# The second layer's state-space stage: order of the next group's preparation

## The chip, the cores and the metric

The kernel runs on one core of one Trainium2 chip. The metric is the time of one execution on the device in microseconds (us), lower is better. A core has four compute engines that run their own instruction queues in order and meet at semaphores: TensorE (PE, with PEld for its weight loads), VectorE (DVE), ScalarE (ACT) and GpSimd (POOL).

## The reference, cut to what matters

The program is a decoder of four layers on 16 sequences of 128 tokens of width 128. The change lies in the first block of the second layer:

```
def _L1_attn_ref(x, ...):
    x_norm = _layernorm(x, ln_g, ln_b)
    x1 = x_norm @ w1_w + w1_b
    u = _silu(_depthwise_conv(x1, conv_w))        # 3 taps along time
    dt = softplus(u @ W_dt + b_dt); Bt = u @ W_B; Ct = u @ W_C
    # for each t, with 16 states n per channel d:
    #   h = exp(dt_t * A) * h + (dt_t * u_t) * B_t
    #   y_t = sum_n h * C_t
    x_ssm = y + u * D_skip
    v = _silu(x_norm @ v1_w + v1_b)
    return x_ssm * v @ w2_w + w2_b
x = _layernorm(x + _L1_attn_ref(x, ...))
```

## The kernel before

`l1_attn` takes the 16 sequences in NG = 4 groups of G = 4, so that a tile is 128 channels by GT = 512 positions. A group has N = 16 states; each is one slot, so that NS = 64 slots run through k, with g = k // 16 and n = k % 16. All loops are written out by hand for each engine; the text order is the queue order.

**A slot.** On TensorE `row_pair(k + 1)` broadcasts the row of B and that of C of the next state into PSUM (lines 3383 and 3387; the B row needs the drive two slots back done, the C row needs ScalarE's copy two slots back), and `add(k - 2)` sums `read` into the PSUM bank `total` (3395, an fp32 product and so two passes). ScalarE copies the C row to SBUF (`c_move`, 3491) and makes the decays exp(dt * A) two slots ahead (`decay_`, 3484, three buffers). VectorE multiplies the B row by `du` (`drive_`, 3563) and scans (`scan`, 3570). GpSimd multiplies the scanned state by the C row (`read_`, 3679). There is one `drive` bank, so drive and scan alternate.

**The preparation of the next group** hangs in fixed slots n of the present one: layer-norm moments on VectorE (`pre_moments`, 3531 and 3533), reciprocal root on GpSimd (`pre_norm`), `pre_scale` on VectorE (3540), transposes on TensorE (`turn_x`, 3336), copy to `xT` (`move_x`, 3439), the convolution as three shifted products and a bias product (`conv`, 3346 and 3349), the gate (`gate`, 3353), their copies into `ug` and a silu over both halves (`move_ug`, 3446 and 3448, and `silu`, 3454), B and C (`bc`, 3359), which are split in three bf16 parts by `split_first` (3457), `split_rest` (3549), `split_mid` (3463, 3464) and `split_low` (3653), and dt (`dt_dot`, 3363; `soften`, 3468 to 3476: bias, absolute value, exponential, logarithm; `softplus_` on VectorE, 3553), at last `du` on GpSimd (`delta_u`, 3659). The functions silu, exponential and logarithm each need their table in ScalarE, and a table load stands in the queue wherever it changes.

**The end of a group** hangs in slots of the next: `skip` (3577) reads `total`, which must be done before the first `add` of the new group may write it; `gated` (3664) on GpSimd; `project_out` (3370, 3371) on TensorE in slots 4 and 5; `moments` and `scale` of the output layer norm on VectorE in slots 7 and 9. The PSUM results of preparation and projection share two banks, `spare`; the list `order` gives who uses which, and a user waits for the release of the one two places ahead.

**Head and tail.** The head prepares group 0 with nothing beside it; the tail finishes group 3. No DMA is issued in the stage.

## Time and profile before

| | us |
|---|---|
| median of 3 runs | 5305.53 |
| lowest and highest run | 5302.63, 5315.38 |
| profiled execution | 5310.23 |
| its span on the core | 5308.4 |
| mean granted clock of TensorE, share of full | 0.91 |
| busy: TensorE, VectorE, ScalarE, GpSimd | 4389.6, 3540.4, 2773.1, 2456.5 |
| the edited stage, from 2239.4 | 232 |

The span is that of the whole program. The stage is read by its own stretches: the first scan starts at 2271.6, the first drive of groups 1, 2 and 3 at 2310.8, 2361.3 and 2412.2, the last scan ends at 2453.6. An idle time in square brackets stands before the instruction that ended it, with who released it. Clock values are shares of full speed; TensorE has the two levels 1.2 and 2.4 GHz (0.50 and 1.00).

### The profile page before, as it was taken

To read this page: it belongs to the slowest core of one execution; us is meant where nothing else is said; L and a number is where in the kernel's file an instruction comes from. 1 tells how busy PE (TensorE), PEld (TensorE's weight loads), DVE (VectorE), ACT (ScalarE), POOL (GpSimd) and SP (SyncE) were. 2 spreads that over 40 slices of the span, in tenths; PEclk is the share of its full clock that TensorE was granted. 3 is DMA by queue.
4 is the path that set the end of the run, shared out by engine and by line. 5 is a ranking of instruction groups with operands and counts; after the bars stand their busy time and mean duration, and the time that the engine had idled before them with its cause. 6 is when DMAs were issued, how large, how long until landed. Compare 5 with 4: busy or idle time off the path is not lost. (4 is left out here: it accounts for less than half of the span.)

```text
span 5308.4 us, 109154 instructions
## 1 busy us (share of the span) xinstructions
PE 4389.6 (83%) x42474; PEld 2700.0 (51%) x42474; DVE 3540.4 (67%) x6848; ACT 2773.1 (52%) x4991; POOL 2456.5 (46%) x2333
## 2 busy tenths in 40 slices
PE   8768999999999999677864888887798879985779
PEld 6545666666666666424632343433365444423445
DVE  4347777777777777476466999999764426646646
ACT  4326676666666666464334656565464415543322
POOL 7536666666665666343044766676533310001100
PEclk9779999999999999877966999999999959996889
DMA  1000100101011000000000000000000000003000
GB/s 24 16 28 15 33 20 21 33 20 29 24 29 24 16 16 20 10 0 2 13 0 15 1 1 0 1 0 1 15 1 1 6 13 6 16 1 75 5 21 7
DMA packets 92006, 76.99 MB, mean 15 GB/s; under 512 B 30999, under 2 KB 74280, under 8 KB 90728
## 3 DMA queue, kind: packets, MB, share of 16 engines
q1 hardware_dynamic: 89447, 68.95, 5.2%
q8 instruction: 342, 5.60, 0.4%
q0 software_dynamic: 2048, 1.05, 0.1%
q14 instruction: 169, 1.38, 0.1%
HBM read 40.18 MB, written 1.18 MB: 8 GB/s over the span
## 5 line engine op out<-in xcount | busy, mean ns | idle before, releaser
L4220 POOL TENSOR_TENSOR l_attn_read<-l_attn_state,l_attn_c_rows 128x1024 f32<-128x1024 f32 x256 | 604.4, 2362 | 291.4 <-DVE l_attn_state L4122 171.6
L2595 PE MATMUL psum<-l_ffn_wq,l_ffn_xsT 128*128 128x512 f32 x1152 | 607.9, 610 | 106.9 <-DVE l_ffn_t L2870 101.5
L3006 POOL TENSOR_TENSOR l_ffn_t<-l_ffn_t 128x512 f32<-128x512 f32 x384 | 486.8, 1268 | 421.3 <-DVE l_ffn_t L2870 416.6
L3842 PE MATMUL psum<-l_attn_read,ident 128*128 128x512 f32 x1024 | 490.6, 597 | 7.7 <-DVE l_attn_yz L4130 5.3
L2866 DVE TENSOR_TENSOR l_ffn_t<-psum,l_ffn_tab 128x512 f32<-128x512 f32 x384 | 260.7, 679 | 326.2 <-ACT l_ffn_sq L2746 307.2
L3012 POOL TENSOR_TENSOR l_ffn_t<-l_ffn_t,l_ffn_ss 128x512 f32<-128x512 f32 x384 | 400.4, 1043 | 62.8 <-DVE l_ffn_ss L2885 62.6
L2746 ACT ACTIVATE l_ffn_sq<-psum 128x512 f32<-128x512 f32 x384 | 225.4, 587 | 290.4 <-PE psum L2595 288.1
L4122 DVE TENSOR_TENSOR_SCAN l_attn_state<-l_attn_decay,psum 128x1024 f32<-128x1024 f32 x144 | 328.9, 2284 | 4.5
L2643 PEld LDWEIGHTS psum<-l_ffn_pT,l_ffn_v 64*64 64x64 f32 x3072 | 231.1, 133 | 167.2 <-ACT l_ffn_pT L2768 132.2
L3998 ACT ACTIVATE l_attn_decay<-l_attn_dt,l_attn_a 128x1016 f32<-128x1016 f32 x256 | 292.9, 1145 | 37.4 <-DVE l_attn_state L4119 34.0
L4023 ACT COPY l_attn_c_rows<-psum 128x512 f32<-128x512 f32 x256 | 149.5, 584 | 297.5 <-PE psum L3833 261.0
L2595 PEld LDWEIGHTS psum<-l_ffn_wq,l_ffn_xsT 128*128 128x128 f32 x1152 | 182.5, 192 | 236.4 <-DVE l_ffn_t L2870 187.3
L2217 ACT ACTIVATE l_attn_pT<-psum 128x512 f32<-128x512 f32 x320 | 173.7, 595 | 243.2 <-PE psum L2115 172.1
L3833 PE MATMUL psum<-l_attn_parts,pick 96*128 96x512 bf16 x456 | 170.1, 390 | 136.8 <-DVE psum L4105 87.9
L4119 DVE TENSOR_TENSOR_SCAN l_attn_state<-l_attn_decay,psum 128x512 f32<-128x512 f32 x224 | 261.7, 1208 | 30.9 <-PE psum L3872 29.0
L2643 PE MATMUL psum<-l_ffn_pT,l_ffn_v 64*64 64x96 f32 (+1 forms) x3072 | 257.6, 233 | 21.2 <-ACT l_ffn_pT L2768 18.9
L3842 PEld LDWEIGHTS psum<-l_attn_read,ident 128*128 128x128 f32 x1024 | 195.7, 193 | 140.6 <-issue 117.0
L4105 DVE TENSOR_TENSOR psum<-psum,l_attn_du 128x1024 f32<-128x1024 f32 x200 | 246.6, 1233 | 26.5 <-POOL l_attn_du L4197 4.6
L2870 DVE TENSOR_TENSOR l_ffn_t<-psum,l_ffn_tab 128x512 f32<-128x512 f32 x384 | 261.4, 681 | 0.0
L2879 DVE TENSOR_REDUCE l_ffn_ss<-l_ffn_sq 128x8 f32<-128x512 f32 x384 | 259.5, 676 | 0.0
L3017 POOL TENSOR_TENSOR l_ffn_p<-l_ffn_p,l_ffn_sm 128x512 f32<-128x512 f32 x192 | 200.1, 1042 | 120.6 <-DVE l_ffn_sm L2902 120.6
L2643 PE MATMUL psum<-l_ffn_pT,l_ffn_vx 64*64 64x96 f32 (+1 forms) x3072 | 255.0, 233 | 0.0
(922 smaller groups left out, 11237.2 us busy)
## 6 DMA issues: line engine op xcount, KB each, us to landing
l_ffn_vx<-l_ffn_v SPq DMA_DIRECT2D x192, 128.0 KB, 2.3
l_ffn_wq<-in_L_ffn_Wqkv SPq DMA_DIRECT2D x6, 1536.0 KB, 6.2
l_xattn_toep<-s4d_taps SPq DMA_DIRECT2D x4, 2048.0 KB, 17.9
l_ffn_wo<-in_L_ffn_Wo SPq DMA_DIRECT2D x6, 512.0 KB, 3.9
l_ffn_w<-in_L_ffn_W SPq DMA_DIRECT2D x6, 341.0 KB
l_ffn_w<-in_L_ffn_w SPq DMA_DIRECT2D x3, 512.0 KB, 4.2
x_all<-in_x SPq DMA_DIRECT2D x4, 256.0 KB, 5.3
l_attn_k<-l_attn_dense_k POOLq DMA_DIRECT2D x64, 16.0 KB, 1.8
```

The lines of the kernel that those rows point to most:

```text
L2595: nc.tensor.matmul(ring[it % 2], xsT[:, n % 2, m % G, :], w, start=True, stop=True).then_inc(itemed, 1)
L2643: last = nc.tensor.matmul(OT[r, i * T + to:i * T + to + n], kinds[par][r, 4 * c + i, :], pT[r, i, at:at + n], start=(to == 0), stop=True, ...
L2866: nc.vector.tensor_tensor(t1[:, m % G, i, :].rearrange("p (h d) -> p h d", d=dh), dots.rearrange("p (h d) -> p h d", d=dh), rows(tab[:, z, ...
L2870: nc.vector.tensor_tensor(t2[:, x % 3, :].rearrange("p (h s d) -> p h s d", s=2, d=32), swapped_halves(dots, 8), tab[:, z, 2 * k + 1, :].r ...
L2879: nc.vector.reduce_sum(ss[:, m % G, 8 * i:8 * i + 8], sq[:, x % 2, :].rearrange("p (h d) -> p h d", d=dh), AX).then_inc(ss_ready, 1)
L3006: nc.gpsimd.tensor_tensor(t1[:, m % G, i, :], t1[:, m % G, i, :], t2[:, x % 3, :], ALU.add).then_inc(added, 1)
L3012: nc.gpsimd.tensor_tensor(t1[:, m % G, i, :].rearrange("p (h d) -> p h d", d=dh), t1[:, m % G, i, :].rearrange("p (h d) -> p h d", d=dh), ...
L3842: last = nc.tensor.matmul(total[:, h * GT:(h + 1) * GT], K.ident[:], read[:, k % 3, h * GT:(h + 1) * GT], start=(n == 0), stop=(n == N - 1 ...
L3998: nc.scalar.activation(decay[:, k % 3, :, :, 1:T], dt[:, g % 2, :].rearrange("p (h g t) -> p h g t", h=2, g=G)[:, :, :, 1:T], ACT.Exp, sca ...
L4119: nc.vector.tensor_tensor_scan(state[:, k % 3, at], decay[:, k % 3, h, :, :].rearrange("p g t -> p (g t)"), drive[:, at], 0.0, ALU.mult, A ...
L4122: nc.vector.tensor_tensor_scan(state[:, k % 3, :], decay[:, k % 3, :, :, :].rearrange("p h g t -> p (h g t)"), drive, 0.0, ALU.mult, ALU.a ...
L4220: nc.gpsimd.tensor_tensor(read[:, k % 3, :].rearrange("p (h n) -> p h n", h=2), state[:, k % 3, :].rearrange("p (h n) -> p h n", h=2), row ...
```

## The change

The preparation of the next group moves within the 16 slots:

| step | slot before | slot after |
|---|---|---|
| moments and reciprocal root of the next group | 0 and 1 | all groups in the head |
| `pre_scale` | 2 | head for group 1, then 13 of the group before |
| transposes, `move_x` | 3, 4 | 0, 1 |
| `conv` on TensorE, copy | 5 and 6, 7 | 1 and 2, 3 |
| `gate`, gate copy and silu | 7, 8 | 3, 4 |
| `dt_dot`, `soften` | 11, 12 | 6, 7 and 8 (logarithm) |
| `softplus_`, `delta_u` | 14, 14 | 10, 10 |
| `bc`, `split_first`, `split_rest`, `split_mid` | 10, 11, 12, 12 | 8, 9, 11, 11 |
| `skip`, `gated` | 3, 3 | 2, 2 |

In the head u gets a silu of its own ahead of the gate's copy, dt comes ahead of B and C, and VectorE makes `du` of group 0. The copy into `ug` waits, from group 2 on, for `gated` of two groups back, whose buffer it takes. The moments' tiles hold 16 sequences in place of 4; `pre_norm` runs twice, over 4 and over 12 of them. The diff, without the bodies of `pre_moments`, `pre_scale` and `pre_norm`, which change in their indices and waits alone:

```diff
...
         spare = (K.bank[6], K.bank[7])
-        order = [("x", 0), ("conv", 0), ("gate", 0), ("parts", 0), ("dt", 0)]
+        order = [(n, 0) for n in ("x", "conv", "gate", "dt", "parts")]
         for g in range(NG):
             if g + 1 < NG:
-                order.append(("x", g + 1))
+                order += [(n, g + 1) for n in ("x", "conv", "gate")]
             if g:
...
             if g + 1 < NG:
-                order += [(n, g + 1) for n in ("conv", "gate", "parts", "dt")]
+                order += [(n, g + 1) for n in ("dt", "parts")]
         order.append(("out", NG - 1))
...
                     ps = claim(use["parts", g])
-                    pe.wait_ge(ug_ready, g + 1)
                     pe.wait_ge(prepared, 2)
...
                 def dt_dot(g):
-                    nc.tensor.matmul(claim(use["dt", g]), wdt[:], ug[:, g % 2, 0, :], start=True, stop=True).then_inc(filled, 1)
+                    ps = claim(use["dt", g])
+                    pe.wait_ge(ug_ready, g + 2 if g else 1)
+                    nc.tensor.matmul(ps, wdt[:], ug[:, g % 2, 0, :], start=True, stop=True).then_inc(filled, 1)
 
...
                 gate(0)
-                bc(0)
                 dt_dot(0)
+                bc(0)
                 row_pair(0)
...
                         continue
-                    if g + 1 < NG and n == 3:
-                        turn_x(g + 1)
+                    if g + 1 < NG:
+                        if n == 0:
+                            turn_x(g + 1)
+                        if n in (1, 2):
+                            conv(g + 1, 2 * (n - 1))
+                            conv(g + 1, 2 * (n - 1) + 1)
+                        if n == 3:
+                            gate(g + 1)
                     if g and n in (4, 5):
...
                     if g + 1 < NG:
-                        if n in (5, 6):
-                            conv(g + 1, 2 * (n - 5))
-                            conv(g + 1, 2 * (n - 5) + 1)
-                        if n == 7:
-                            gate(g + 1)
-                        if n == 10:
-                            bc(g + 1)
-                        if n == 11:
+                        if n == 6:
                             dt_dot(g + 1)
+                        if n == 8:
+                            bc(g + 1)
                 for i in range(G):
...
                     ps = take(n)
+                    if g >= 2:
+                        act.wait_ge(y_ready, g - 1)
                     if i == 0:
...
 
+                def silu_first(i):
+                    wait_moved(act, use[("conv", "gate")[i], 0])
+                    nc.scalar.activation(ug[:, 0, i, :], ug[:, 0, i, :], ACT.Silu).then_inc(ug_ready, 1)
+
                 def silu(g):
...
 
-                def soften(g):
+                def soften(g, i):
                     n = use["dt", g]
-                    nc.scalar.activation(dt[:, g % 2, :], take(n), ACT.Identity, bias=cl[:, 3:4]).then_inc(moved[n % 2], 1)
...
+                    if i == 0:
+                        nc.scalar.activation(dt[:, g % 2, :], take(n), ACT.Identity, bias=cl[:, 3:4]).then_inc(moved[n % 2], 1)
...
+                        nc.scalar.activation(tmp[:], tmp[:], ACT.Exp, scale=-1.0).then_inc(soft_step, 1)
+                    else:
+                        act.wait_ge(soft_step, 3 * g + 2)
+                        nc.scalar.activation(tmp[:], tmp[:], ACT.Ln, bias=1.0).then_inc(soft_step, 1)
...
                 move_ug(0, 0)
+                silu_first(0)
                 move_ug(0, 1)
-                silu(0)
+                silu_first(1)
+                soften(0, 0)
                 split_first(0)
+                soften(0, 1)
                 split_mid(0)
-                soften(0)
                 act.wait_ge(prepared, 3)
...
                     if g + 1 < NG:
-                        if n == 4:
+                        if n == 1:
                             move_x(g + 1)
-                        if n == 7:
+                        if n == 3:
                             move_ug(g + 1, 0)
-                        if n == 8:
+                        if n == 4:
                             move_ug(g + 1, 1)
                             silu(g + 1)
-                        if n == 11:
+                        if n == 7:
+                            soften(g + 1, 0)
+                        if n == 8:
+                            soften(g + 1, 1)
+                        if n == 9:
                             split_first(g + 1)
-                        if n == 12:
+                        if n == 11:
                             split_mid(g + 1)
-                            soften(g + 1)
 
...
                 nc.vector.tensor_scalar(a[:], a[:], -1.0, None, ALU.mult).then_inc(prepared, 1)
+                for g in range(1, NG):
+                    pre_moments(g)
+                pre_scale(1)
                 split_rest(0)
                 softplus_(0)
+                dve.wait_ge(dt_ready, 1)
+                nc.vector.tensor_tensor(du[:, 0, :], dt[:, 0, :], ug[:, 0, 0, :], ALU.mult).then_inc(du_ready, 1)
                 for k in range(NS):
...
                     drive_(k)
-                    if g + 1 < NG:
-                        if n == 0:
-                            pre_moments(g + 1)
-                        if n == 2:
-                            pre_scale(g + 1)
                     if g:
-                        if n == 3:
+                        if n == 2:
                             skip(g - 1)
...
                     if g + 1 < NG:
-                        if n == 12:
-                            split_rest(g + 1)
-                        if n == 14:
+                        if n == 10:
                             softplus_(g + 1)
+                        if n == 11:
+                            split_rest(g + 1)
+                    if g + 2 < NG and n == 13:
+                        pre_scale(g + 2)
                     scan(k)
...
                 pre_norm(0)
+                pre_norm(1)
                 split_low(0)
-                delta_u(0)
                 for k in range(NS):
                     g, n = k // N, k % N
-                    if g + 1 < NG and n == 1:
-                        pre_norm(g + 1)
                     read_(k)
                     if g:
-                        if n == 3:
+                        if n == 2:
                             gated(g - 1)
...
                     if g + 1 < NG:
+                        if n == 10:
+                            delta_u(g + 1)
                         if n == 12:
                             split_low(g + 1, k)
-                        if n == 14:
-                            delta_u(g + 1)
                 gated(NG - 1)
```

On TensorE, from slot 3 of group 1 on before, with the projection of group 0 (3370, 3371) behind the transposes (3336):

```order
L3383 MATMUL psum<-l_attn_parts,pick 128x512
L3387 MATMUL psum<-l_attn_parts,pick 128x512
L3395 MATMUL psum<-l_attn_read,ident 128x512
L3336 MATMUL psum<-ident,l_attn_xn 128x128 x4
L3383 MATMUL psum<-l_attn_parts,pick 128x512
L3387 MATMUL psum<-l_attn_parts,pick 128x512
L3395 MATMUL psum<-l_attn_read,ident 128x512
L3370 MATMUL psum<-l_attn_w,l_attn_yz 128x128
L3371 MATMUL psum<-l_attn_b,ones 128x128
```

Now, from slot 0 of group 1 on; `xTp` and `wk` are the convolution's input and taps:

```order
L3384 MATMUL psum<-l_attn_parts,pick 128x512
L3388 MATMUL psum<-l_attn_parts,pick 128x512
L3396 MATMUL psum<-l_attn_read,ident 128x512
L3336 MATMUL psum<-ident,l_attn_xn 128x128 x4
L3384 MATMUL psum<-l_attn_parts,pick 128x512
L3388 MATMUL psum<-l_attn_parts,pick 128x512
L3396 MATMUL psum<-l_attn_read,ident 128x512
L3346 MATMUL psum<-l_attn_xTp,l_attn_wk 128x512 x2
L3384 MATMUL psum<-l_attn_parts,pick 128x512
```

The transposes and the first two taps now stand ahead of the group's own first `add`, which follows this piece (the two 3396 here sum the last states of group 0). Line numbers of the changed kernel are higher by 1 to 15.

On ScalarE, slots 12 and 13 of group 0 before; `low` and `parts` are the split of B and C, `dt` and `tmp` the softplus:

```order
L3491 COPY l_attn_c_rows<-psum 128x512
L3484 ACTIVATE l_attn_decay<-l_attn_dt,l_attn_a 128x4x127
L3463 CAST l_attn_low<-l_attn_rest 32x512
L3464 CAST l_attn_parts<-l_attn_rest 32x512
L3468 ACTIVATE l_attn_dt<-psum,l_attn_cl 128x512
L3472 ACTIVATE l_attn_tmp<-l_attn_dt 128x512
L3474 ACTIVATE l_attn_tmp<-l_attn_tmp 128x512
L3476 ACT_TABLE_LOAD
L3476 ACTIVATE l_attn_tmp<-l_attn_tmp 128x512
L3491 COPY l_attn_c_rows<-psum 128x512
L3484 ACT_TABLE_LOAD
L3484 ACTIVATE l_attn_decay<-l_attn_dt,l_attn_a 128x4x127
```

Now, slots 7 to 9:

```order
L3477 ACTIVATE l_attn_dt<-psum,l_attn_cl 128x512
L3481 ACTIVATE l_attn_tmp<-l_attn_dt 128x512
L3483 ACTIVATE l_attn_tmp<-l_attn_tmp 128x512
L3501 COPY l_attn_c_rows<-psum 128x512
L3494 ACTIVATE l_attn_decay<-l_attn_dt,l_attn_a 128x4x127
L3486 ACT_TABLE_LOAD
L3486 ACTIVATE l_attn_tmp<-l_attn_tmp 128x512
L3501 COPY l_attn_c_rows<-psum 128x512
L3494 ACT_TABLE_LOAD
L3494 ACTIVATE l_attn_decay<-l_attn_dt,l_attn_a 128x4x127
L3465 CAST l_attn_parts<-psum 96x512
```

The seven instructions of one slot are now spread over slots 7 to 11, with C's copy and a decay between them.

On VectorE, head before, from the negated `a` to the first scan:

```order
L3611 TENSOR_SCALAR l_attn_a<-l_attn_a 128x16
L3549 TENSOR_TENSOR l_attn_rest<-psum,l_attn_parts 96x512
L3553 SCALAR_TENSOR_TENSOR l_attn_dt<-l_attn_dt,l_attn_tmp 128x512
L3563 TENSOR_TENSOR psum<-psum,l_attn_du 128x512
L3531 BN_STATS l_attn_pre_stats<-x_all 128x6 x4
L3533 BN_AGGR l_attn_pre_mean<-l_attn_pre_stats 128x2 x4
L3570 SCALAR_TENSOR_TENSOR l_attn_state<-l_attn_decay,psum 128x512
```

Now, from the last moments to the first drive:

```order
L3544 BN_STATS l_attn_pre_stats<-x_all 128x6 x4
L3546 BN_AGGR l_attn_pre_mean<-l_attn_pre_stats 128x2 x4
L3554 TENSOR_SCALAR l_attn_xn<-x_all,l_attn_pre_mean,l_attn_pre_rstd 128x128 x4
L3563 TENSOR_TENSOR l_attn_rest<-psum,l_attn_parts 96x512
L3567 SCALAR_TENSOR_TENSOR l_attn_dt<-l_attn_dt,l_attn_tmp 128x512
L3632 TENSOR_TENSOR l_attn_du<-l_attn_dt,l_attn_ug 128x512
L3577 TENSOR_TENSOR psum<-psum,l_attn_du 128x512
```

The moments left the place between the first drive and the first scan, and `du` is VectorE's.

## Rows read from the trace of the kernel before

**Rows 1.** Busy time by stretch: the head and the four groups.

```profile
core 0: us, PE busy (x) PEld busy (x) DVE busy (x) ACT busy (x) POOL busy (x), PEclk, DMA share, GB/s
2239.40:2271.60 32.20, 15.29 (x24) 4.86 (x24) 7.58 (x37) 16.43 (x21) 5.97 (x7) 0.55 0.00 0
...
2271.60:2310.80 39.20, 31.44 (x78) 11.92 (x78) 33.01 (x39) 31.52 (x48) 22.67 (x20) 0.86 0.00 1
...
2310.80:2361.30 50.50, 37.01 (x98) 15.21 (x97) 39.35 (x60) 31.50 (x48) 26.23 (x24) 0.83 0.00 0
...
2361.30:2412.20 50.90, 37.52 (x100) 15.61 (x99) 39.35 (x61) 31.60 (x48) 26.32 (x24) 0.83 0.00 0
...
2412.20:2453.60 41.40, 30.93 (x79) 11.87 (x78) 35.10 (x46) 17.78 (x29) 22.57 (x19) 0.87 0.00 1
```

**Rows 2.** Timeline of VectorE, group 1: start and duration in us, instruction, [idle before].

```profile
2313.01 1.19 DVE L3570 TENSOR_TENSOR_SCAN l_attn_state<-l_attn_decay,psum 128x512 f32<-128x512 f32 x1
...
2314.31 0.70 DVE L3563 TENSOR_TENSOR psum<-psum,l_attn_du 128x512 f32<-128x512 f32 x1
...
2316.37 0.70 DVE L3563 TENSOR_TENSOR psum<-psum,l_attn_du 128x512 f32<-128x512 f32 x1
...
2318.87 1.21 DVE L3570 TENSOR_TENSOR_SCAN l_attn_state<-l_attn_decay,psum 128x512 f32<-128x512 f32 x1
...
2324.19 0.70 DVE L3563 TENSOR_TENSOR psum<-psum,l_attn_du 128x512 f32<-128x512 f32 x1 [1.52 <-PE psum L3383]
...
2334.86 0.70 DVE L3563 TENSOR_TENSOR psum<-psum,l_attn_du 128x512 f32<-128x512 f32 x1 [2.72 <-PE psum L3383]
...
2337.79 1.19 DVE L3570 TENSOR_TENSOR_SCAN l_attn_state<-l_attn_decay,psum 128x512 f32<-128x512 f32 x1
...
2361.33 0.70 DVE L3563 TENSOR_TENSOR psum<-psum,l_attn_du 128x512 f32<-128x512 f32 x1 [1.78 <-PE psum L3383]
```

**Rows 3.** Waits in the stage, 2230 to 2480 us: total, times, longest.

```profile
DVE psum L3563 <- PE psum L3383: 19.3, 13, 2.7
...
DVE l_attn_dt L3553 <- ACT l_attn_tmp L3476: 10.9, 4, 6.6
...
DVE psum L3563 <- POOL l_attn_du L3659: 5.1, 3, 1.8
```

**Rows 4.** Timeline of TensorE in groups 1 and 3.

```profile
2321.68 2.04 PE L3395 MATMUL psum<-l_attn_read,ident 128*128 128x512 f32 x2 [6.01 <-DVE l_attn_yz L3577]
...
2327.34 1.02 PE L3395 MATMUL psum<-l_attn_read,ident 128*128 128x512 f32 x2
...
2327.77 0.19 PEld L3370 LDWEIGHTS psum<-l_attn_w,l_attn_yz 128*128 128x128 f32 x1 [0.24 <-issue]
...
2329.76 0.39 PE L3383 MATMUL psum<-l_attn_parts,pick 96*128 96x512 bf16 x1
...
2358.28 0.63 PE L3383 MATMUL psum<-l_attn_parts,pick 96*128 96x512 bf16 x1
...
2360.84 0.46 PE L3383 MATMUL psum<-l_attn_parts,pick 96*128 96x512 bf16 x1
...
2442.61 1.80 PE L3395 MATMUL psum<-l_attn_read,ident 128*128 128x512 f32 x2
```

**Rows 5.** Timeline of the head, all engines.

```profile
2253.04 0.58 ACT L3446 COPY l_attn_ug<-psum 128x512 f32<-128x512 f32 x1 [6.58 <-PE psum L3349]
...
2259.96 0.69 DVE L3549 TENSOR_TENSOR l_attn_rest<-psum,l_attn_parts 96x512 f32<-96x512 f32 x1 [14.92 <-ACT l_attn_parts L3457]
...
2261.37 1.15 POOL L3653 TENSOR_TENSOR l_attn_parts<-l_attn_rest,l_attn_low 32x512 bf16<-32x512 f32 x1 [18.04 <-ACT l_attn_low L3463]
...
2263.32 1.28 ACT L3474 ACT_TABLE_LOAD   x1
...
2264.62 0.63 ACT L3474 ACTIVATE l_attn_tmp<-l_attn_tmp 128x512 f32<-128x512 f32 x1
...
2271.63 1.19 DVE L3570 TENSOR_TENSOR_SCAN l_attn_state<-l_attn_decay,psum 128x512 f32<-128x512 f32 x1
```

More of the change, by code:

```diff
@@ L3285, in l1_attn @@
         xn = sb("xn", [128, G, D])
[L3286 to L3288 removed]
+        pre_stats = sb("pre_stats", [128, NB, 6])
+        pre_mean = sb("pre_mean", [128, NB, 2])
+        pre_rstd = sb("pre_rstd", [128, NB])
         xT = sb("xTp", [128, G, T + TAPS - 1])
```

62 lines of the change are left out of this document (27 added, 35 removed).

## The prediction

> **What bounds the kernel now.** The page comes first: a span of 5308.4 us over all four layers, of which the edited stage is a small part. The view of busy time by stretch then gives its size [rows 1]: a head of 32.2 us, four groups of 39.2, 50.5, 50.9 and 41.4 us, and a tail of 18.1 us. In the groups VectorE is busy 33.0 of 39.2, 39.4 of 50.5, 39.4 of 50.9 and 35.1 of 41.4 us. No other engine sets the pace on average, though TensorE is close behind (37.0 of 50.5 us, at a mean granted clock of 0.83 of full speed). A slot on VectorE is a drive product (0.70) and a scan (1.19 to 1.22); undisturbed, drive follows drive after 2.06 us (2314.31 to 2316.37) [rows 2]. So 64 slots are 132 us, and the most that better order can win is the waits and extras between them.
>
> The view of waits says who stops VectorE [rows 3]: B's rows from TensorE (19.3 us in 13 waits), the logarithm for the softplus from ScalarE (10.9, of which 6.6 in the head), `du` from GpSimd (5.1 in 3). The timeline of group 1 shows where [rows 2]: four waits, 1.52 to 2.72 us at the ends, before the drives of slots 4 to 7 (6.3 us in all), and 1.78 before the next group; one of 1.31 before the softplus lies between. The first four have one origin. TensorE stood idle for 6.01 us until `skip` in slot 3 had read the total [rows 4], was then at half clock (1.2 GHz, a pair of passes in 2.04 us against 1.02 later at 2.4 GHz), and had projection and convolution to do in the same slots. Group 2 repeats this (six waits, 9.7 us); group 3, with only the projection, has four waits of 4.5 us.
>
> **The change part by part.** I count each stretch anew: undisturbed VectorE time plus the waits I still expect. A scan starts 0.73 us after its drive; what more it takes is the extra's price [rows 2]: `pre_moments` 1.5 (2310.8 to 2313.01), `pre_scale` 1.8 (2316.37 to 2318.87), output moments 2.2 (2334.86 to 2337.79); `scale`, four operations of the same kind as `pre_scale`, 1.8; `skip`, `split_rest` and softplus, one 512-column operation each, 0.6.
>
> *Head.* The new ScalarE queue is convolution copy, table load, silu of u, gate copy, silu of gate, then dt. From the copy's start at 2253.04 [rows 5]: copy 0.58, load 1.28, half a silu 0.63 (as the 128x512 exponential at 2264.62) gives 2255.55; the dt product at half clock, 2.04 [rows 4], gives 2257.6; bias, absolute value, load, exponential 0.69 + 0.63 + 1.28 + 0.63 gives 2260.85; first rounding of B and C 0.58, load and logarithm 1.91 give 2263.3. The low part needs 0.61 on ScalarE and 1.15 on GpSimd (2265.15), the first B row 0.58 and its drive 0.70 (2266.45); ScalarE's second cast, load and decay end at 2266.6. Softplus and `du`, now on VectorE (0.69 each), end at 2264.8 and are covered. The first scan starts at 2266.65 against 2271.63: **5.0 us won**, with 1.5 either way for the new interleaving. The moments of the three other groups (3 x 1.7) and one `pre_scale` lie on a VectorE that waits 14.92 us there [rows 5]: free; should that cover be missing, 7 us.
>
> *Group 0.* Clean: 15 x 2.06 + 1.33 to the next group's first drive, + 0.6 + 0.6 + one `pre_scale` 1.78 = 35.2 us. The waits for softplus (1.68) and `du` (1.77) go, since both are made by slot 10. New waits come on TensorE. In slot 1 it stands before the convolution until ScalarE has moved xT (after two decays and two C rows, about 2270.8), in front of B's row of slot 3. The two taps cost 1.7 us at full clock and 3.4 at half, so that row comes 1.0 or 2.8 us late, and the tap and bias of slot 2 cost 1.3 to 3.7 more. Bounds 2.3 and 6.5. Before, TensorE came to full clock some 8 us after its first row, in group 0; the new order has it at work from 2265 on, so that about half of the excess remains: 3.6. Sum 38.8 against 39.2: **0.4 won**.
>
> *Group 1.* Clean: 16 x 2.06 = 33.0, skip 0.6, moments 2.2, scale 1.8, 0.6 + 0.6, `pre_scale` of group 3 1.78: 40.6. `skip` comes a slot earlier and the pre-moments are gone, so TensorE waits for the total some 3 us less. Following the queues from the last scan's end: xT moved at 3.5, two taps to 5.2, first `add` 5.6 to 6.5 (`skip` ends at 5.45), tap and bias to 8.3, B of slot 4 at 8.7 (due 8.8), gate to 10.5, half the projection to 13.8 (1.99 us a slot, 2327.77 to 2329.76 [rows 4]), so B of slot 6 is 1.2 us late, and B of slot 7 again 1.2. That is 2.4 us at full clock; if the group starts at half clock, as before at 2321.68, about 6. The light slots speak for some of that: in group 3 a pair of passes took 1.80 us at 2442.61, after `scale` on VectorE had left TensorE without work [rows 4]. I take 3.5. Sum 44.1 against 50.5: **6.4 won**.
>
> *Group 2.* The same without `pre_scale`: 38.8 + 3.5 = 42.3 against 50.9: **8.6 won**.
>
> *Group 3.* 32.9 + 0.6 + 2.2 + 1.8 = 37.5; the projection alone fits in the slack (bounds 0 and 1.0, I take 0.5): 38.0 against 41.4: **3.4 won**.
>
> *Added wait.* From group 2 on, the copy of the convolution into `ug` waits for `gated` two groups back. It can start at about 7.4 after the last scan; GpSimd ends read and gate at 6.7 + 1.27 + 1.27 = 9.3. So ScalarE stands 1.9 us, with C's row of slot 4 and a decay behind it. The decay of slot 7, after the silu and its two loads, ends at 16.9 and is due at about 18: covered by 1 to 3 us of run-ahead. Uncovered it is in the first rival. Tail and head's first half are unchanged: 0.
>
> **Sum:** 5.0 + 0.4 + 6.4 + 8.6 + 3.4 = 23.8 us. The profiled execution took 5310.2 (span 5308.4), 4.7 above the median of the runs, 5305.5, which itself lies between 5302.6 and 5315.4. 5305.5 - 23.8 = 5281.7. With all TensorE waits at their low ends (2.3 + 2.4 + 2.4 + 0 = 7.1 instead of 11.1) and the head at its best it is 29.3 us, with all at their high ends (6.5 + 6 + 6 + 1 = 19.5) and the head at its worst 13.9.
>
> A page against a row. In the trace a table load takes 1.28 us, no idle time stands before it, and the next activation starts 1.30 after it (2263.32, 2264.62) [rows 5]. The Trainium skill, ScalarE: Activation LUTs, What ACT_TABLE_LOAD costs, adds 1.38 us of drain to the 1.28. That is a sentence on the page alone: by it the four loads of a group would make ScalarE 5.5 us busier, and the clumps in slots 4 and 8 would reach the scans; I would estimate some 8 us less gain, about 5290 (an estimate from the page's figure). The rows speak against it.
>
> **Rivals.** *The wait moves to ScalarE.* Silu, gate copy and two loads now fall in slots 3 to 5, where TensorE, too, is fullest, and in groups 1 and 2 the new wait precedes them. If `gated` ends a slot and a half later than I count (3 us), the decay of slot 7 and C's row of slot 5 are late, TensorE, which takes its rows in order, holds B back, and some 5 us are lost in each of groups 1 and 2 and 3 in group 0: gain 23.8 - 13 = 10.8, 5294.7. For it: ScalarE's work in a group, 31.5 us [rows 1], nearly fills group 0's 35. Against: before, the same clump in slot 8 of group 0 cost VectorE 0.23 us.
>
> *The change doesn't do what it says in the groups:* TensorE's waits only change slots, and there remain the head (5.0), two `pre_moments` inside groups 1 and 2 and one `pre_scale` (4.7): 9.7, 5295.8.
>
> *Slower: TensorE at half clock throughout.* Spread out, its work might never be dense enough. At half clock a slot's B, C and add take 2.56 us (2358.28 to 2360.84) [rows 4], more than VectorE's 2.06: 64 x 2.56 = 164; preparation is 6.8 us at full clock (eight passes of convolution and bias and six of gate, dt and B/C at 0.43, since a pair of 1.02 is one pass and the 0.59 of the last, and 0.8 of transposes), the projection 4.0, so at half clock 2 x (3 x 6.8 + 3 x 4.0) = 65: 229 us in place of 182 for the groups, less 5 in the head: +42, 5347.5. The kernel becomes slower from a half-clock share of about 0.6 on; before it was 0.34 (clock 0.83), and in the light slots of group 3 it returned to full by itself.
>
> **Chances.** Forecast 0.76; wait moves to ScalarE 0.12; waits only change slots 0.05; half clock 0.04; the page's drain 0.03. A difference of 0.3% (16 us) is about what a measurement of this kernel can tell from no change. The forecast's own range has a gain of 14 to 29, so a small part of it counts as no change: faster 0.76, same 0.19, slower 0.05. The range reaches from 5270 (gain 29 and the scatter of the runs, some 6) to 5298 (both small rivals and a little scatter); it leaves out the half clock and a gain beyond 35.
>
> **What would show it.** First scan 5 us earlier after the stage's start; no wait of VectorE before softplus or the first drive of a group; TensorE's 6 us before the first add of a group down to about 3 or less; the waits for B's rows moved from slots 4 to 7 to slots 6 and 7 and, in group 0, 3 and 4, with 11 us in all where there were 19; groups of about 38.8, 44, 42 and 38 us. Wrong would be: VectorE waiting for a decay in slots 6 to 8, a granted clock in the groups clearly under 0.83, or a gain outside this stage.

## The result and the profile after

| | before | after |
|---|---|---|
| median of 20 runs each, us | 5305.48 | 5298.08 |
| lowest and highest run | 5294.9, 5322.8 | 5283.92, 5308.18 |
| ratio after/before | | 0.9979 [0.9971, 0.9986] |
| profiled execution, its span | 5310.23, 5308.4 | 5292.65, 5290.9 |

The forecast was 5281.7, with a range of 5270 to 5298. The medians differ by 7.4 us, the ratio gives 11 (7 to 15), and the forecast gain was 23.8. Of all executions in this document two, one of e6 with 6980 us and one of e8 with 13029, were in a slow state and are left out of the ratios. The changed stage did what was forecast. The view of busy time by stretch, kernel after, with the borders at the first scan and at the first drives of the groups as in [rows 1]; columns are the stretch, its length, busy time and count of each engine, granted clock of TensorE, DMA share and GB/s:

```profile
core 0: us, PE busy (x) PEld busy (x) DVE busy (x) ACT busy (x) POOL busy (x), PEclk, DMA share, GB/s
2242.00:2269.60 27.60, 13.71 (x22) 4.91 (x23) 13.34 (x58) 14.89 (x20) 7.26 (x8) 0.62 0.00 0
2269.60:2308.90 39.30, 32.25 (x82) 12.38 (x81) 33.69 (x38) 32.03 (x50) 21.39 (x18) 0.88 0.00 1
2308.90:2351.80 42.90, 35.05 (x98) 13.57 (x97) 38.74 (x53) 31.91 (x48) 25.13 (x22) 0.94 0.00 1
2351.80:2392.60 40.80, 36.67 (x100) 14.60 (x98) 36.61 (x49) 31.83 (x48) 25.07 (x22) 0.89 0.00 0
2392.60:2430.50 37.90, 30.16 (x77) 11.09 (x76) 34.99 (x46) 18.27 (x29) 22.56 (x19) 0.86 0.00 1
```

| us | before | forecast | after |
|---|---|---|---|
| head, to the first scan | 32.2 | 27.2 | 27.6 |
| group 0 | 39.2 | 38.8 | 39.2 |
| group 1 | 50.5 | 44.1 | 42.9 |
| group 2 | 50.9 | 42.3 | 40.8 |
| group 3 | 41.4 | 38.0 | 38.0 |
| tail, to the start of VectorE's last instruction | 15.5 | 15.5 | 16.0 |
| stage | 229.5 | 205.7 | 204.5 |

(The parts were read to 0.1 us; those of the first two columns add up to 0.2 more than the stage. The kernel after's were read from the starts of the instructions, the borders of the view are rounded.) The stage won 25.0 us. A second execution of each kernel, traced in the experiments, gave 229.5 and 204.5 again. So the missing gain, 25 less 11 or some 14 us, is not in the changed stage.

What changed length is the next stage, the second layer's cross-attention. I measure it from the start of VectorE's last instruction in the changed stage to its first in the feed-forward stage behind. Before it took 175.6 us, after 179.6 in the profiled execution, and 196.8 in the second traced one. That is 12.6 us more on the mean of the two, near the missing 14. The two profiled executions add up: -25.0 in the stage, +4.0 in the cross-attention, +2.6 ahead of the stage and +1.0 from the feed-forward stage on make the difference of the spans, 5308.4 and 5290.9, within the rounding. No code changed outside the stage.

One execution's total does not show the loss, however. What lies ahead of the stage took 2242.0 and 2227.6 us in the two traces of after, and everything outside the stage and the cross-attention 4906.8 and 4881.9 (before: 4903.3 and 4904.3). Such a scatter is as large as the gain. So single traces are used for the stages alone, and the whole kernels are compared by their ratios.

Inside the stage, the waits of VectorE in the kernel after, 2230 to 2460 us (total, times, longest), against [rows 3]:

```profile
DVE l_attn_rest L3563 <- ACT l_attn_parts L3465: 8.5, 2, 8.1
DVE psum L3577 <- PE psum L3384: 7.7, 13, 1.4
DVE y L3597 <- PE psum L3372: 7.4, 1, 7.4
```

B's rows now cost 7.7 us in 13 waits where they cost 19.3, and no drive waits for `du`. By group the 7.7 are 1.9, 2.4, 2.4 and 0.8, with 0.2 ahead of the first drive. The timeline of VectorE, kernel after, head and groups 0 and 1 (start, duration, instruction, [idle before]), shows where:

```profile
2266.25 0.69 DVE L3567 SCALAR_TENSOR_TENSOR l_attn_dt<-l_attn_dt,l_attn_tmp 128x512 f32<-128x512 f32 x1 [1.25 <-ACT l_attn_tmp L3486]
2266.98 1.65 DVE L3632 TENSOR_TENSOR l_attn_du<-l_attn_dt,l_attn_ug 128x512 f32<-128x512 f32 x1
...
2269.63 1.22 DVE L3584 TENSOR_TENSOR_SCAN l_attn_state<-l_attn_decay,psum 128x512 f32<-128x512 f32 x1
...
2278.60 0.70 DVE L3577 TENSOR_TENSOR psum<-psum,l_attn_du 128x512 f32<-128x512 f32 x1 [1.35 <-PE psum L3384]
...
2286.24 1.22 DVE L3584 TENSOR_TENSOR_SCAN l_attn_state<-l_attn_decay,psum 128x512 f32<-128x512 f32 x1 [0.67 <-ACT l_attn_decay L3494]
...
2322.88 0.70 DVE L3577 TENSOR_TENSOR psum<-psum,l_attn_du 128x512 f32<-128x512 f32 x1 [0.91 <-PE psum L3384]
...
2325.74 0.70 DVE L3577 TENSOR_TENSOR psum<-psum,l_attn_du 128x512 f32<-128x512 f32 x1 [0.91 <-PE psum L3384]
```

In group 1 the two larger waits stand before the drives of slots 6 and 7. The timeline of TensorE, kernel after, start of group 1, against [rows 4]:

```profile
2309.04 0.60 PE L3336 MATMUL psum<-ident,l_attn_xn 128*128 128x128 f32 x4
...
2312.34 1.96 PE L3346 MATMUL psum<-l_attn_xTp,l_attn_wk 128*128 128x512 f32 x4 [1.08 <-issue]
...
2314.57 1.02 PE L3396 MATMUL psum<-l_attn_read,ident 128*128 128x512 f32 x2
```

The `add` at 2314.57 is the group's first. The 6.01 us of idle time ahead of it are gone, and it runs at full clock, 1.02 us a pair of passes where it had 2.04. The timeline of ScalarE, kernel after, group 2:

```profile
2361.00 0.58 ACT L3450 COPY l_attn_ug<-psum 128x512 f32<-128x512 f32 x1 [1.90 <-POOL l_attn_yz L3679]
...
2363.45 1.28 ACT L3462 ACT_TABLE_LOAD   x1
2364.74 1.06 ACT L3462 ACTIVATE l_attn_ug<-l_attn_ug 128x1024 f32<-128x1024 f32 x1
```

The added wait for `gated` is 1.90 us long and reaches no scan. The activation starts 1.29 after the table load, with no drain that shows.

### The profile page after: what moved, and what is told of

Read it like the earlier page. It is cut to its first block and busy times, and to the rows that moved or that the text cites. A ratio compares the mean times of both kernels' runs of the same rounds, so it can differ in the third digit from the quotient of the medians.

```text
span 5290.9 us, 109154 instructions
## 1 busy us (share of the span) xinstructions
PE 4394.5 (83%) x42474; PEld 2703.3 (51%) x42474; DVE 3539.5 (67%) x6849; ACT 2773.2 (52%) x4992; POOL 2454.3 (46%) x2328
## 3 DMA queue, kind: packets, MB, share of 16 engines
q14 instruction: 168, 1.38, 0.1%
```

## The experiments

All kernels below ran in five rounds beside the kernel before. Where one has added work, its result is unused and the outputs are the same. "Cross-attention" is the stretch defined above, read in one traced execution of each.

### Both kernels again

`e1_before_again` and `e2_after_again` are the two kernels unchanged. The expectations count the stage up to the next one's first instruction on VectorE, 2.8 us further than the tables here.

> The kernel before, unchanged, as a second sample of its trace. The edited stage (from the first moments of the stage to the first VectorE instruction of the next) took 232.3 us before and 207.3 us after in the two traces at hand, 25.0 less, while the medians of 20 runs differ by 7.4 us and their means by 10.3. Theory A (the stage is always about 25 us shorter and the rest of the program pays some 15 of it back): here stage 232 within 1.5, rest of the program 5074 to 5078. Theory B (the stage's own gain changes from run to run with the granted clock of TensorE, and the traced pair was a good one): stage anywhere from 222 to 233. Ratio to the kernel before 1.000 by both.

> The changed kernel, unchanged, as a second sample of its trace. Theory A: stage 207 within 1.5, rest of the program 5083 or more, against about 5076 in traces of the kernel before. Theory B: stage 207 to 222, rest within 3 us of that of the kernel before. Ratio 0.998 by both.

Measured: before again 1.0003 [0.9993, 1.0013]; after again 0.9977 [0.9964, 0.999]. The same two sizes come again, and the stage is the same to 0.1 us, so that its gain doesn't vary with the execution (theory B). But theory A missed, too: it wanted 5083 us or more for the rest of the program in after again, and the rest took 5076.0 (5083.6 in the first trace of after), since what lies ahead and behind was shorter in this execution. The view of busy time by stretch, from the start of the cross-attention, cut at 42, 74 and 94 us. Kernel before again:

```profile
2469.90:2511.90 42.00, 33.46 (x192) 24.71 (x192) 21.06 (x32) 8.52 (x14) 0.00 (x0) 0.50 0.02 6
2511.90:2543.90 32.00, 30.39 (x462) 24.50 (x460) 18.71 (x34) 15.61 (x28) 0.00 (x0) 1.00 0.01 2
2543.90:2563.90 20.00, 18.97 (x266) 14.90 (x263) 11.10 (x26) 8.61 (x19) 1.66 (x4) 1.00 0.01 2
2563.90:2645.50 81.60, 69.12 (x885) 52.00 (x883) 34.96 (x84) 32.26 (x63) 5.06 (x13) 0.91 0.01 2
```

Kernel after, the profiled execution:

```profile
2446.50:2488.50 42.00, 33.40 (x192) 24.72 (x192) 21.11 (x32) 8.46 (x14) 0.00 (x0) 0.54 0.02 6
2488.50:2520.50 32.00, 30.36 (x436) 24.07 (x432) 18.03 (x33) 14.21 (x26) 0.00 (x0) 0.93 0.01 2
2520.50:2540.50 20.00, 19.25 (x272) 15.04 (x264) 9.97 (x24) 8.86 (x18) 1.66 (x4) 0.99 0.01 2
2540.50:2626.20 85.70, 72.95 (x911) 54.87 (x907) 36.68 (x87) 33.68 (x66) 5.05 (x13) 0.88 0.01 2
```

Kernel after again:

```profile
2432.10:2474.10 42.00, 33.38 (x192) 24.72 (x192) 21.10 (x32) 8.49 (x14) 0.00 (x0) 0.54 0.02 6
2474.10:2506.10 32.00, 32.00 (x284) 26.98 (x282) 11.67 (x21) 8.84 (x16) 0.00 (x0) 0.50 0.00 1
2506.10:2526.10 20.00, 19.26 (x234) 14.49 (x231) 10.50 (x19) 9.77 (x17) 0.00 (x0) 0.91 0.01 2
2526.10:2629.00 102.90, 89.62 (x1093) 68.30 (x1091) 43.10 (x104) 38.20 (x76) 6.72 (x17) 0.85 0.01 2
```

In the first 42 us all three do the same: 192 products, 33.4 us busy, at 1.2 GHz nearly throughout. The 0.54 instead of 0.50 of the two traces of after is one short rise, in the first 12 us, before again and then after again:

```profile
2469.70:2481.70 12.00, 4.76 (x8) 1.88 (x8) 7.96 (x12) 2.70 (x5) 0.00 (x0) 0.50 0.07 20
```

```profile
2432.10:2444.10 12.00, 4.71 (x8) 1.89 (x8) 7.96 (x13) 2.83 (x5) 0.00 (x0) 0.60 0.07 20
```

In after again the clock was full from 2441.6 to 2445.0, while TensorE stood idle ahead of its first small products (2445.43), which then ran at half clock as before. So this rise won nothing, but it is the first difference between the two. At 42 us before goes to full clock and does 462 products in 32 us. After again stays at 1.2 GHz, TensorE is busy 32.00 of 32 us and does only 284. After, in the execution of the first section, rose, was at half clock once more later, and lost 4 us. The groups of TensorE's instructions (busy us, mean ns) in that second stretch, before again and then after again, show one kind of product at either level (neighbours overlap, so busy time is less than count times mean):

```profile
L892 PE MATMUL psum<-l_xattn_k,l_xattn_q 32*128 32x120 f32 x139 | 18.3, 282 | 0.7 <-DVE l_xattn_q L1115 0.7
```

```profile
L892 PE MATMUL psum<-l_xattn_k,l_xattn_q 32*128 32x120 f32 x92 | 20.7, 435 | 0.0
```

So TensorE sets the pace in these stretches (busy 30.4 to 32.0 of 32 us), the cross-attention starts at half clock in both kernels, and its length goes with when the clock rises and whether it stays up. This loss is of the size of the missing gain. Why the clock rose later is the question of the runs from here on.

### The two halves of the change

`e3_head_only` has the changed head, with all moments and the `pre_scale` of group 1 in it, and the loops of before; `e4_loops_only` has the changed loops and the old order of the head on TensorE, ScalarE and GpSimd, but the moments still in the head.

```diff
 # e3_head_only, on the kernel after (TensorE's queue; the others likewise)
-                    if g + 1 < NG:
-                        if n == 0:
-                            turn_x(g + 1)
+                    if g + 1 < NG and n == 3:
+                        turn_x(g + 1)
...
-                        if n == 6:
-                            dt_dot(g + 1)
-                        if n == 8:
+                        if n == 10:
                             bc(g + 1)
+                        if n == 11:
+                            dt_dot(g + 1)
```

> Only the head of the stage is changed: dt ahead of B and C, silu in two, du of group 0 on VectorE, moments of all groups and pre_scale of group 1 in the head; the loops keep the slots of before, without the moments. My sum: first scan 5 us earlier, three moments of 1.5 us and one pre_scale of 1.8 us less in the loops: stage 232.3 - 11.3 = 221. Rival (TensorE or ScalarE is late anyway behind the moments that go): only the head counts, 227 to 229. Whole kernel by theory A: 5 us less than before at most, since part is paid back elsewhere; by theory B about 9 to 11 less.

```diff
 # e4_loops_only, on the kernel after
-                silu_first(0)
                 move_ug(0, 1)
-                silu_first(1)
-                soften(0, 0)
+                silu(0)
                 split_first(0)
-                soften(0, 1)
                 split_mid(0)
+                soften(0, 0)
+                soften(0, 1)
```

> The loops of the changed kernel with the head's old order of dt, B and C (the moments stay in the head). My sum: 5 us of head less gained than in the changed kernel: stage 207.3 + 5 = 212. Rival (group 0's waits on TensorE get shorter when TensorE is at work later, so the head's gain was partly given back in group 0): 209 to 210. Whole kernel: theory A about 3 us above the changed kernel, theory B 5.

| us | before | e3 | e4 | after |
|---|---|---|---|---|
| first scan after the stage's start | 32.2 | 27.6 | 30.8 | 27.6 |
| group 0 | 39.2 | 37.5 | 42.3 | 39.2 |
| group 1 | 50.5 | 47.8 | 43.2 | 42.9 |
| group 2 | 50.9 | 47.8 | 40.8 | 40.8 |
| group 3 | 41.4 | 40.8 | 38.0 | 38.0 |
| tail | 15.5 | 14.5 | 15.8 | 16.0 |
| stage | 229.5 | 215.9 | 210.9 | 204.5 |
| cross-attention | 175.6 | 193.1 | 191.0 | 179.6, 196.8 |
| ratio to before | 1 | 0.9985 [0.9972, 0.9997] | 0.9984 [0.9974, 0.9993] | 0.9979 |

Both halves work. The first won 13.6 us where 11.3 had been expected (the text on record counts the stage up to the next one's first instruction, 232.3 before): moments and `pre_scale` taken out of group 0 gave 1.7, moments out of groups 1 and 2 gave 2.7 and 3.1. With the loops already changed, the head's order gives 6.4 where 5 had been expected: 3.2 in the head and 3.0 in group 0. The rival for e4, that group 0 gives part of it back, is thus wrong. The loops in their turn cost group 0 1.8 us (37.5 to 39.2, rounded) and win 4.9, 7.0 and 2.8 in the others. The program gained much less than the stage in both, 8 to 9 us by the ratios (for e3 5 at most had been expected), and the cross-attention took 15 to 18 us longer in the traced executions. So the loss hangs on neither half.

### Starting the next stage later

If the moment at which the cross-attention starts decides its clock, a small delay should change its length by far more than the delay. `e5_after_later` puts 1.5 us of sums behind the last instruction of the changed stage on VectorE; `e14_after_later_again` is the same kernel. `e10_plus06`, `e11_plus30` and `e12_plus50` have one, five and eight sums.

```diff
+                nc.vector.tensor_tensor(du[:, 0, :], dt[:, 0, :], dt[:, 1, :], ALU.add)
+                nc.vector.tensor_tensor(du[:, 1, :], dt[:, 0, :], dt[:, 1, :], ALU.add)
+                nc.vector.tensor_tensor(tmp[:, 0:256], dt[:, 0, 0:256], dt[:, 1, 0:256], ALU.add)
```

> The changed kernel with three idle-time operations more on VectorE at the very end of the stage (two sums over 512 columns, one over 256, results unused), so that the next stage starts 1.5 us later. Traces so far: the stage takes 229.5 us before and 204.5 changed (first to last VectorE instruction, two traces each), and the cross-attention stage behind it 175.6 and 175.6 before, 179.6 and 196.8 changed, 193.1 head only, 191.0 loops only; its clock rises to 2.4 GHz for good 42 us after the stage's end before, between 74 and 94 us in the others. Theory A1 (when the cross-attention starts decides how long its clock stays at 1.2 GHz, and the old start was a lucky one): stage 206.0, cross-attention somewhere else than 180 to 197, possibly 176, and then the whole kernel about 10 us under the changed one. Theory A2 (the shorter stage leaves TensorE in another state at its end, whatever the start): cross-attention again 180 to 197, whole kernel 1.5 us slower than the changed one.

> The changed kernel with one sum over 512 columns at the stage's end, 0.6 us. Theory A1: the lucky start was reached by 1.5 us, and the start of the kernel before lies there too; 0.6 us is in between, so that runs mix: cross-attention 176 to 197, kernel 5290 to 5299. Rival (any delay helps): 175.7, 5289.

> The changed kernel with five such sums, 3.0 us. Theory A1: as far behind the lucky start as the changed kernel is ahead of it (1.5 us), cross-attention 180 to 197, as with 1.9 us of delay on the kernel before (191.3), kernel 5297 to 5305. Rival (any delay helps): 175.7, kernel 5291.

> The changed kernel with eight such sums, 5.0 us. If the price of a start repeats with the start (early, lucky, late, lucky again), the cross-attention may be back at 176, kernel near 5293; if only one start was lucky, 180 to 197, kernel 5300 or more.

> The kernel after with three sums on VectorE (two of 512 columns, one of 256, unused results, 1.5 us) behind the last instruction of the second layer's state-space stage, a second time. Theory A (the stage's gain is kept where the cross-attention starts at this moment): cross-attention 175.7 us as the first time, stage 206.0, kernel 5288 to 5291, ratio 0.9957 to 0.997. Theory C (chance): cross-attention anywhere between 176 and 209 us, kernel 5289 to 5311.

The same was done to the kernel before, with three sums in `e6_before_later` and with five and a smaller one in `e13_before_plus34`.

> The kernel before with three such sums over 512 columns, 1.9 us, at the end of the stage. Theory A1: the cross-attention leaves its lucky start: 180 to 197 in place of 175.6, so that 1.9 us of delay cost 6 to 23 us. Theory A2, and plain addition: 175.6 again, whole kernel 1.9 us slower, ratio 1.0004.

> The kernel before with five sums of 512 columns and one of 256 on VectorE (96 partitions, unused results) after the last instruction of the second layer's state-space stage, which starts the cross-attention about 3.4 us later than before does; that is the same distance as between the kernel after with 1.5 us and the kernel after with 5.0 us of such sums, both of which had a cross-attention of 176 us. State-space stage 229.5 + 3.4 = about 233. Theory A (good starts come again after about this distance, whatever the stage ahead of them): cross-attention 175 to 177 us, full clock from about 42 us on, kernel only 3 to 4 us slower than before, ratio 1.0007. Theory B (the start of before was a single good one): cross-attention 180 to 209 us, kernel 8 us or more slower, ratio 1.0015 or more. Theory C (the start has nothing to do with it, the length of the cross-attention differs from program to program by chance): no value is favoured.

| kernel | added, us | stage | cross-attention | ratio to before |
|---|---|---|---|---|
| after | 0 | 204.5 | 179.6, 196.8 | 0.9979 [0.9971, 0.9986] |
| e10 | 0.6 | 204.8 | 203.1 | 1.001 [0.9997, 1.0022] |
| e5 | 1.5 | 206.0 | 175.7 | 0.9957 [0.9945, 0.9969] |
| e14 | 1.5 | 205.9 | 175.6 | 0.9967 [0.9955, 0.9979] |
| e11 | 3.0 | 207.2 | 208.7 | 1.0007 [0.9995, 1.0018] |
| e12 | 5.0 | 209.1 | 175.9 | 0.997 [0.9958, 0.9983] |
| before | 0 | 229.5 | 175.6, 175.6 | 1 |
| e6 | 1.9 | 231.3 | 191.3 | 1.0012 [0.9998, 1.0025] |
| e13 | 3.4 | 233.1 | 175.8 | 1.0006 [0.9996, 1.0016] |

The view of busy time by stretch for the kernel with 1.5 us (e5), whole cross-attention, cut as above:

```profile
2448.40:2490.40 42.00, 33.40 (x192) 24.70 (x192) 21.15 (x32) 8.46 (x14) 0.00 (x0) 0.50 0.02 6
2490.40:2522.40 32.00, 30.39 (x460) 24.43 (x458) 18.71 (x34) 15.59 (x28) 0.00 (x0) 1.00 0.01 2
2522.40:2542.40 20.00, 18.96 (x265) 14.90 (x264) 10.99 (x26) 8.63 (x18) 1.66 (x4) 1.00 0.01 2
2542.40:2624.10 81.70, 69.21 (x885) 52.08 (x885) 35.05 (x84) 32.35 (x63) 5.05 (x13) 0.91 0.01 2
```

and its second and third stretch for 3.0 us (e11):

```profile
2494.70:2526.70 32.00, 32.00 (x290) 26.70 (x281) 11.59 (x21) 9.13 (x17) 0.00 (x0) 0.50 0.01 1
2526.70:2546.70 20.00, 19.26 (x188) 14.11 (x188) 7.62 (x14) 8.31 (x14) 0.00 (x0) 0.67 0.01 2
```

With 1.5 us more the kernel after has the cross-attention of before, stretch for stretch, and is 6 to 12 us faster by the ratios than after. With 0.6 or 3.0 us it loses the whole gain of the stage. e10, e11 and e12 ran beside each other on one chip, so that no difference of chips stands behind theirs; e5 and e14 ran on two others and are compared through the ratios. Before, too, loses with 1.9 us, though less in the runs (6 us by the ratio, its interval just reaching 1) than in the one trace (17.5), and with 3.4 us has its 175.8 back and pays only for the delay.

Not all of this had been forecast. The expectations had 176 to 197 us for e10 and 180 to 197 for e11, and both kernels faster than they were. That good starts should come again was said for e12 as a possibility and for e13 as theory A, and both came out so.

The traces can be held against the runs. Stage and cross-attention together differ from before's 405.1 us by -23.4 in e5, -23.6 in e14, -20.1 in e12 and +3.8 in e13; the ratios give -23, -18, -16 and +3 us. Where the cross-attention was long, one trace fits less well: +17.5 against +6 in e6, +3.9 against -8 in e3, +10.8 against +4 in e11. The length may well change there from execution to execution, as it did in after; e5 and e14 had only five executions each, which lie some 9 us apart; the 29 and 17 of before beside them lie 21 and 29 us apart.

That the length differs by chance from execution to execution is ruled out for e5 by e14. That each program has a length of its own, by its layout and not by its start, is made unlikely by e13 alone, one forecast that came true, where 7 of 16 traces (e8 among them) have such a length. All delays were made by sums on VectorE; none by other means.

The short rise in the first 12 us can be looked up in every trace. The clock was full once, between 9 and 14 us into the cross-attention, in both traces of after and in e4, e6, e9 and e11, whose cross-attention took 179.6 to 208.7; it stayed at 1.2 GHz for the first 42 us in before, e1, e5, e12, e13 and e14, all of them at 176. But e3 and e10 had no such rise either and took 193.1 and 203.1. So it goes with the loss and doesn't account for all of it.

The start that counts is not the time since the program's start: e5 and e14 came to the stage 8.7 us apart (2242.4 and 2233.7) and had the same cross-attention.

### A delay in the head, and a control

`e9_head_later` delays VectorE at the start of the changed stage instead.

```diff
+                nc.vector.memset(yz[:], 0.0)
+                nc.vector.memset(du[:, 0, :], 0.0)
+                nc.vector.memset(du[:, 1, :], 0.0)
+                nc.vector.memset(tmp[:, 0:256], 0.0)
```

> The changed kernel with four memsets more on VectorE (three of 512 columns, one of 256, results unused) at the start of the stage, about 1.4 us, in place of the sums at its end. With the sums at the end the stage took 206.0 us, the cross-attention 175.7, the kernel 5289.5. Theory A1 (the moment at which the cross-attention starts decides): 1.4 us more of stage, cross-attention near 176 here too, kernel near 5290. Rival (something in the sums at the end, such as what they do to the stage's last us on the other engines): cross-attention 180 to 197, kernel near 5299.

Measured: `pre_scale` was pushed by 1.58 us, but the first scan was not (27.4) and the stage took 204.3: the head's waits swallowed it. Cross-attention 196.9, ratio 0.9996 [0.998, 1.0013]. Relative to the stage, the delay did not reach the next one, so it says nothing on delays; but it is a control. Four more instructions of VectorE, without a longer stage, don't bring the 175.7 us back.

### More work for TensorE

Two kernels tried to raise the clock. `e7_after_busy_tail` has ten unused products of 512 columns behind the stage's last projection, `e8_after_dense_scores` eight ahead of the first scores in the cross-attention.

```diff
 # e7_after_busy_tail
+                pe.wait_ge(driven, NS)
+                for i in range(10):
+                    nc.tensor.matmul(b_bank[0], K.ident[:], read[:, 0, :], start=True, stop=True)
```

> The changed kernel with ten products of 128x128x512 more on TensorE behind the last projection (results unused), where it stands idle for about 7.5 us. It enters the cross-attention at 2.4 GHz. Theory A2 or any in which the clock at the entry decides: the first 40 us of the cross-attention run at twice the speed, stage 155 to 165. Theory A1 (the small products of the cross-attention, 32 rows of the array each, don't hold the clock): it falls back within 10 us, cross-attention 175 to 197 as before. The stage itself grows by 0 to 3 us.

```diff
 # e8_after_dense_scores
+                    if not local and t == 6:
+                        for i in range(8):
+                            nc.tensor.matmul(O, K.ident[:], K.x_all[:, 12:16, :], start=True, stop=True)
```

> The changed kernel with eight products of 128x128x512 more on TensorE inside the cross-attention, ahead of its first scores (results unused). If full-width work raises the clock and the scores keep it: cross-attention 150 to 165 and the kernel 20 us faster. If the scores don't keep it: 7 us of extra work at 1.2 GHz, some of it under other engines' work, cross-attention 180 to 204.

Busy time by stretch, the start of the cross-attention with ten products ahead (e7):

```profile
2445.80:2455.00 9.20, 6.75 (x19) 2.84 (x17) 0.95 (x6) 0.00 (x1) 0.00 (x0) 1.00 0.00 1
2455.00:2485.00 30.00, 23.80 (x114) 18.02 (x116) 16.12 (x21) 5.05 (x8) 0.00 (x0) 0.51 0.03 8
```

The clock did rise and was full for the first 9.2 us. It fell at 2455.4, while TensorE stood idle for 2.6 us between the transposes and the product for the queries, and so 9.5 us before the first small product (2464.87). The cross-attention took 200.4, the ratio is 1.0008 [0.9993, 1.0023]. Full clock at the entry alone thus doesn't help; whether the small products would have kept it, e7 doesn't show.

e8 does. The start of its cross-attention:

```profile
2436.80:2445.00 8.20, 3.22 (x7) 1.82 (x8) 4.37 (x9) 0.58 (x1) 0.00 (x0) 0.50 0.10 29
2445.00:2455.00 10.00, 9.89 (x34) 4.77 (x33) 5.48 (x8) 2.67 (x4) 0.00 (x0) 0.94 0.01 2
2455.00:2479.00 24.00, 23.91 (x155) 18.50 (x159) 11.14 (x18) 4.34 (x8) 0.00 (x0) 0.53 0.00 1
```

The eight products began at 2446.23, the clock was full from 2446.1, the first small products began at 2453.20 at full clock, and at 2456.4 it fell with TensorE at work (busy 23.91 of 24 us). The cross-attention took 176.8 in this execution, with full clock again from 43.5 us on, but the ratio, 0.9989 [0.9975, 1.0003], is no better than that of after. For the time of the kernel I take e8 as inconclusive.

## Why the prediction was wrong

**The step that failed** is the subtraction 5305.5 - 23.8. It took all that lies behind the stage as unchanged. I had read where TensorE's clock stood in the edited stage, and never looked at the next one, where TensorE sets the pace and begins at 1.2 GHz. There a start that is moved by 25.0 us, or by 0.6 to 5.0 less, costs anything from 0 to 33 us in the traces (175.6 to 208.7). In the runs, 11 us were left of the stage's 25.0 (by the ratio). "A gain outside this stage" was named as what would be wrong; it was a loss. The lower bound of the gain, 14 us, rested on terms of the stage alone, and the range up to 5298 on these, the two small rivals in the stage and the scatter of the runs.

**The head: 5.0 forecast, 4.6 measured.** The queue came as written; the logarithm ended 24.2 us after the stage's start instead of 23.8, and what hangs on it came as much later. `du` on VectorE took 1.65 us instead of 0.69, which cost nothing: the first drive still waited 0.22 us behind it for B's row. The cover for the three moments and `pre_scale` held.

**Group 0: 38.8 forecast, 39.2 measured.** Waits of 3.6 were forecast on TensorE's side. They were 1.9 for B's rows (the largest 1.35 before slot 4), 0.7 for a decay and 0.9 and 0.3 for softplus and `split_rest`: another split of nearly the same sum, 3.8, and so partly luck. The wait for softplus, which was to go, had 0.9 of its 1.68 us left.

**Groups 1 and 2: 3.5 of waits each forecast, 2.4 measured.** I had taken the value between 2.4 (full clock) and 6 (half) on the strength of a light slot. The row at 2314.57 shows full clock from the first `add`; the low end was right. Of the four waits the larger two are before slots 6 and 7, as followed through the queues, 0.91 each where 1.2 had been forecast. Against the sums the groups were another 0.1 and 0.4 shorter. That the stage came out at 204.5 for 205.7 is in part luck, too: head, group 0 and tail were 1.3 longer, these two groups 2.7 shorter.

**Group 3: 38.0 forecast, 38.0 measured**, with one wait of 0.8 for 0.5.

**The added wait** was forecast at 1.9 us and covered. It measured 1.90, and no scan of group 2 waited for a decay. One scan of group 0 did, 0.67 us; that is small, but it is the decay of slot 7 that the first rival named.

**The tail** was forecast unchanged and took 0.5 more. The first pair of the projection there, before and after:

```profile
2459.13 0.46 PE L3370 MATMUL psum<-l_attn_w,l_attn_yz 128*128 128x128 f32 x2 [2.27 <-POOL l_attn_yz L3664]
```

```profile
2436.01 0.77 PE L3371 MATMUL psum<-l_attn_w,l_attn_yz 128*128 128x128 f32 x2 [2.27 <-POOL l_attn_yz L3679]
```

The clock fell before the projection instead of within it. It is no sign of what happened behind: in e5 the same pair takes 0.77 us, and the cross-attention 175.7.

**The rivals.** Their mechanisms did not occur in the stage: neither the late decays (0.67 us for a loss of 13), nor waits that only changed slots (7.7 for 19.3), nor half clock throughout (0.86 to 0.94 in the groups), nor a drain of the table loads (1.29 us from the load's start to the activation's). The Trainium skill, ScalarE: Activation LUTs, What ACT_TABLE_LOAD costs, has 1.38 us of drain beside the load, and no row shows that. That the result of 5298.1 lies near two of them, 5294.7 and 5295.8, is a coincidence of sums.

**What stays open.** Shown is that 1.5 us of sums at the border of the two stages win 6 to 12 us by the ratios (for e5 the interval lies below that of after, for e14 the two overlap by 0.0008), that 5.0 us win about as much, and that 0.6 and 3.0 lose. That they act by the moment of the start is argued from e9 and e13. Not shown is what makes a start favourable, or why one kernel (after) had 179.6 and 196.8 in two executions with the same stage. The first 42 us of before and of after again don't differ in TensorE's work, only in the short rise of the clock. A trace shows one execution, so the sizes in the runs don't follow it closely (e6, e8).

**The better kernel.** After with 1.5 us of unused sums at the stage's end ran at 5289.52 and 5284.75 us (before beside them 5310.44 and 5302.28) and has lower medians than both kernels. It keeps the stage's gain by a delay that fits this program only; the lasting form would be a cross-attention less sensitive to its start, which was not tried.

## What to carry to other kernels

Before a stage's gain is subtracted from the whole, read the stretches behind it: where TensorE sets the pace there and begins at 1.2 GHz, as here, a shift of the start can cost as much as the change won. Compare stage by stage and not only the total, and if a later stage without any edit has another length, test it with a small delay at its border before the change is blamed. A wait bounded between two clock levels was decided here by the idle time ahead of it that the change removed.

## What the runs showed of the hardware

Small fp32 products with 32 rows took 282 ns at 2.4 GHz and 435 at 1.2 GHz, and TensorE stayed at the lower level for a whole stretch in which it was busy 32.00 of 32 us. A TensorE busy in the trace had not brought the clock up. From the same work the rise came at 42 us in before, e1, e5, e12, e13 and e14, at 78 to 80 us in after again, e4, e6 and e9, and at 95 in e10; in after and e3 it came at 42, and the clock fell back once. Sums of 0.6, 1.5, 3.0 and 5.0 us ahead of its start gave 203.1, 175.7, 208.7 and 175.9 us, not in the order of their size. A full clock fell in 2.6 us of idle time in e7, and in e8 3.2 us after the first of these products, with TensorE at work. And `du` on VectorE, 128x512, took 1.65 us where the softplus product of the same size just ahead took 0.69; an instruction of GpSimd of 1.15 us began 0.05 us before it.
